# Six chained attention blocks on one core: the 128-row matmuls and transposes become pairs of 64-row ones, and all eight PSUM banks form one ring

## What is computed

```python
qp = (q @ Wq.T + bq).reshape(-1, H, seq, HD)       # kp, vp from the context
scores = jnp.einsum('bhqd,bhkd->bhqk', qp, kp)     # masks set scores to -inf
attn = jax.nn.softmax(scores / sqrt(HD), axis=-1)
out = jnp.einsum('bhqk,bhkd->bhqd', attn, vp).reshape(-1, seq, D)
y = x + out @ Wo.T + bo                            # then a layer norm
...
h = act(x @ w1.T + b1); y = x + h @ w2.T + b2      # 256 -> 1024 -> 256 in blocks 1 and 5
```

## Time and profile before

| | |
|---|---|
| median of 3 runs | 2486.88 us (2486.25 to 2492.78) |
| the profiled execution | 2489.72 us, of which the span from first to last instruction 2487.9 us |
| PE busy | 2393.9 us, 24352 matmuls |
| DVE busy | 1926.6 us |
| ACT busy | 1454.0 us |
| POOL busy | 1104.9 us |
| mean granted TensorE clock | 0.991 of full speed |

### The profile page before, as it was taken

The page is one execution under the profiler, slowest core; times in us unless marked ns, Lnnn a source line. Parts: engine busy times, 40 slices in busy tenths (PEclk is TensorE's granted clock), DMA queues, the critical chain, the costliest instruction groups (busy, mean ns, idle before and its releaser), DMA issues.

```text
span 2487.9 us, 63230 instructions
## 1 busy us (share of the span) xinstructions
PE 2393.9 (96%) x24352; PEld 1855.5 (75%) x24352; DVE 1926.6 (77%) x4308; ACT 1454.0 (58%) x2321; POOL 1104.9 (44%) x1606
## 2 busy tenths in 40 slices
PE   5999999999999989999999999999999999999997
PEld 4766767688888868878776666667777778888886
DVE  6888988877778877777788888878789876666662
ACT  1444444565555544455556677677677777666664
POOL 1333434444444433455445677786445443222220
PEclk8999999999999999999999999999999999999998
DMA  5453343222111111232222322222422221111120
GB/s 168 107 157 89 98 102 81 94 75 67 63 63 63 63 43 48 76 106 87 89 92 94 98 92 83 72 82 91 136 93 99 99 76 63 63 63 63 59 84 13
DMA packets 138379, 208.55 MB, mean 84 GB/s; under 512 B 43857, under 2 KB 52321, under 8 KB 138082
## 3 DMA queue, kind: packets, MB, share of 16 engines
q1 hardware_dynamic: 113506, 201.03, 24.7%
q0 software_dynamic: 24576, 3.49, 1.1%
HBM read 40.70 MB, written 4.19 MB: 18 GB/s over the span
## 4 chain that ended last, share of the span: by engine, by line
PE 68%; DVE 9%; issue 2%; ACT 1%; POOL 1%; DMA 0%; DVEq 0%; ACTq 0%
PE ps_pv L854 9%; PE ps_st L677 8%; PE ps_nat L659 7%; PE ps_misc L770 5%; PE ps_misc L886 3%; DVE mx L1307 3%; PE ps_misc L809 3%; PE ps_misc L919 3%; PE ps_misc L954 2%; PE ps_misc L903 2%; PE ps_misc L865 2%; PE ps_misc L955 2%; PE ps_misc L956 2%; PE ps_misc L921 2%; PE ps_misc L920 2%
## 5 line engine op out<-in xcount | busy, mean ns | idle before, releaser
L1037 ACT ACTIVATE pt<-ps_st 128x1024 f32<-128x1024 f32 (+1 forms) x768 | 760.3, 990 | 656.2 <-PE ps_st L677 367.4
L1428 POOL DMA_DIRECT2D q_st<-shifts_t x768 | 456.4, 599 | 1062.7 <-DVE shifts_t L1319 1062.2
L1307 DVE TENSOR_REDUCE mx<-ps_nat 128x4 f32<-128x1024 f32 x560 | 679.8, 1214 | 185.0 <-PE ps_nat L659 166.6
L659 PE MATMUL ps_nat<-k_st,q_st 64*128 64x256 f32 (+1 forms) x3072 | 353.8, 308 | 36.2 <-DVE mx L1307 20.1
L677 PE MATMUL ps_st<-q_st,k_st 64*128 64x256 f32 (+1 forms) x3072 | 366.5, 317 | 10.0 <-ACT pt L1037 6.2
L854 PE MATMUL ps_pv<-pt,vaug 128*32 128x256 f32 (+1 forms) x6144 | 374.5, 376 | 0.0
L677 PEld LDWEIGHTS ps_st<-q_st,k_st 64*128 64x128 f32 x3072 | 231.5, 185 | 145.2 <-issue 106.3
L659 PEld LDWEIGHTS ps_nat<-k_st,q_st 64*128 64x128 f32 x3072 | 233.4, 186 | 111.3 <-issue 63.9
L854 PEld LDWEIGHTS ps_pv<-pt,vaug 128*32 128x32 f32 x6144 | 171.8, 110 | 124.2 <-ACT pt L1037 7.1
L1086 ACT ACTIVATE hT<-ps_misc,cols 128x256 f32<-128x256 f32 x288 | 121.3, 477 | 130.3 <-PE ps_misc L921 72.4
L919 PE MATMUL ps_misc<-xF_hi,up_hi 128*128 128x256 f32 x512 | 158.1, 309 | 14.1 <-DVE qk L1185 10.9
(11 more groups left out here) (159 smaller groups left out, 5061.5 us busy)
## 6 DMA issues: line engine op xcount, KB each, us to landing
q_st<-qk SPq DMA_DIRECT2D x576, 128.0 KB
k_st<-qk SPq DMA_DIRECT2D x576, 128.0 KB, 2.1
q_st<-shifts_t POOLq DMA_DIRECT2D x768, 4.0 KB, 1.8
weights<-in_weights SPq DMA_DIRECT2D x19, 512.0 KB, 4.0
cT<-in_ctx_t SPq DMA_DIRECT2D x32, 256.0 KB, 2.8
cn<-in_ctx SPq DMA_DIRECT2D x32, 256.0 KB, 2.7
xT<-in_x_t SPq DMA_DIRECT2D x16, 256.0 KB, 3.2
xn<-in_x SPq DMA_DIRECT2D x16, 256.0 KB, 3.0
```

What stands on the lines that cost most here:

```text
L659: return nc.tensor.matmul(ps_nat[:, j, hf, 0:keys], lhs, rhs, start=hf == 0, stop=last)
L1037: nc.scalar.activation(pt[:, g % PT_SLOTS, :, 0:used], ps_st[:].rearrange("p j a b -> p j (a b)")[:, :, 0:used], ACT.Exp, scale=SCALE).the ...
L1307: last = nc.vector.reduce_max(out, ps_nat[:], AX)
L1428: nc.gpsimd.dma_start(rows[:, b], shifts_t[32 * b:32 * b + 32, i, :]).then_inc(split_in[rot][i], 16)
```

## The change

Every step named in `WIDE` now takes two neighbouring banks, and its matmuls are 64-row ones.

- `both_rows` replaces a 128-row matmul into one half of the output by two 64-row matmuls, on rows 0 to 63 and on rows 64 to 127. They write to different banks, so in part 0 rows 0 to 63 add into half 0 and rows 64 to 127 into half 1. In part 1 the two are swapped. Part 1 first waits (`rows_done`) until the last matmul of part 0 is done.
- `both_turns` replaces a transpose of 128x128 by two of 64 rows each, with 64 columns moved in place of 128.
- `ff2a` and `ff2` do the same over four parts, with a `rows_done` wait ahead of the second and the fourth.
- `otr` stays 128\*128 in blocks 2 and 3; `pvg` and `e0` stay 128\*32.
- The four PSUM tensors become one, `ps`, of eight banks. `Order` hands out banks, or pairs of neighbouring banks, oldest first, to all steps alike. `nat`, `st` and `pvg` are among them. PE waits for whatever step held the banks last.
- Readers take both banks with one access (two runs of 256, or blocks of 64). For `otr` of blocks 0, 1, 4 and 5 DVE now needs two reciprocals of 8 elements for one of 16, and four multiplications of 64 elements for one of 256 (blocks 1, 4, 5) or two of 128 (block 0).
- `STEPS` has new numbers throughout.

```diff
-MISC = 3
+BANKS = 8
+WIDE = {"nat": range(NA), "st": range(NA), "pq": (0, 1, 2, 3, 4, 5), "pk": (0, 1, 2, 3, 4, 5), "pvv": (0, 1, 2, 3, 4, 5), "opr": (0, 1, 4, 5),
+        "ff1": (1, 3, 5), "ff2": (1, 3, 5), "ff2a": (1, 5),
+        "xtr": (1, 2, 3, 4, 5), "xff": (1, 3, 5), "ctr": (3, 5), "otr": (0, 1, 4, 5), "ott": (1, 4, 5), "pvt": (0,)}
...
-    0: [("ldt", 0, -23.0722), ("pq", 0, -10.5145, {"a": -11.9187}), ("pql", 0, -10.1072), ("pk", 0, -8.6981, {"a":
+    0: [("ldt", 0, -15.0949), ("pq", 0, -11.609, {"q": -10.7939, "a": -10.4052}), ("pql", 0, -9.8317), ("pk", 0, -10.5429,
...
-                bank = next(b for b in turn if b not in held.values())
-                turn.remove(bank)
-                turn.append(bank)
+                taken = {b for banks in held.values() for b in banks}
+                age = {b: k for k, b in enumerate(turn) if b not in taken}
+                if wide(e):
+                    first = min((b for b in age if b + 1 in age), key=lambda b: (max(age[b], age[b + 1]), b))
+                    banks = [first, first + 1]
+                else:
+                    banks = [min(age, key=age.get)]
...
                 def open_bank(e, part=None):
-                    bank, count = win.bank[e]
-                    if count > 1 and part != 1:
-                        pe.wait_ge(misc_out[bank], count - 1)
-                    return ps_misc[:, bank, :]
+                    if part == 1 and wide(e):
+                        pe.wait_ge(rows_done, phases[e])
+                    if part != 1:
+                        for old in win.before[e]:
+                            if old[0] == "nat":
+                                pe.wait_ge(max_done, nth(old))
+                            elif old[0] == "st":
+                                pe.wait_ge(exp_done, nth(old))
+                            else:
+                                wait_out(pe, old)
+                    return ps[:, win.bank[e][0], :]
+
+                def both_turns(e, c, src):
+                    if not wide(e):
+                        return nc.tensor.transpose(ps[:, win.banks[e][0], P * c:P * c + P], src, ident[:])
+                    for g in range(2):
+                        rows = slice(GROUP * g, GROUP * g + GROUP)
+                        last = nc.tensor.transpose(ps[:, win.banks[e][g], GROUP * c:GROUP * c + GROUP], src[rows], ident[rows, rows])
+                    return last
+
+                def both_rows(e, swap, lhs, rhs, start, stop):
+                    out = halves_of(e)
+                    if not wide(e):
+                        return nc.tensor.matmul(out[:, swap, :], lhs[swap], rhs[swap], start=start, stop=stop)
+                    for g in range(2):
+                        half, rows = g ^ swap, slice(GROUP * g, GROUP * g + GROUP)
+                        last = nc.tensor.matmul(out[:, half, :], lhs[half][rows], rhs[half][rows], start=start and not swap,
+                                                stop=stop and bool(swap))
+                    return last
+
+                def half_done(e, last):
+                    phases[e] = len(phases) + 1
+                    last.then_inc(rows_done, 1)
...
-            for c in halves:
-                out, cut = bank[:, c * S:(c + 1) * S], slice((2 * i + c) * P, (2 * i + c + 1) * P)
-                for dk in range(2):
-                    nc.tensor.matmul(out, up_hi[dk][:, cut], xF_hi[:, dk, :], start=dk == 0, stop=False)
...
+            for dk in range(2):
+                w_hi, w_lo = [up_hi[dk][:, cut] for cut in cuts], [lo[:, dk, cut] for cut in cuts]
+                both_rows(e, part, w_hi, [xF_hi[:, dk, :]] * 2, dk == 0, False)
...
-                        link(nc.vector.reciprocal(rec[:, i], bank[:, :, :, HD]))
+                            for hf in range(2):
+                                last = nc.vector.reciprocal(own[:, hf], bank[:, hf, :, :, :, HD])
+                            link(last)
...
+                                for g in range(2):
+                                    src, by = bank[:, hf, :, g, :, 0:HD], own[:, hf, :, g].unsqueeze(3).to_broadcast([P, 2, 2, HD])
...
+                                    last = nc.vector.tensor_tensor(dst, src, by, ALU.mult)
```

More of the change, by code:

```diff
@@ L212, in plan @@
     return out
-MISC_KINDS = ("pq", "pk", "pvv", "pvt", "ctr", "e0", "otr", "ott", "opr", "xtr", "xff", "ff1", "ff2a", "ff2")
-RELEASE = {"len": "e0", "pql": "pq", "pkl": "pk", "xtl": "xtr", "xfl": "xff"}
+IN_BANKS = ("nat", "st", "pvg", "pq", "pk", "pvv", "pvt", "ctr", "e0", "otr", "ott", "opr", "xtr", "xff", "ff1", "ff2a", "ff2")
+RELEASE = {"pvout": "pvg", "len": "e0", "pql": "pq", "pkl": "pk", "xtl": "xtr", "xfl": "xff"}
 class Order:
@@ L230, in __init__ @@
         halved = {e for e, *_ in self.by["q"]}
-        self.kinds, self.bank = {}, {}
+        self.kinds, self.bank, self.banks, self.before, self.ready = {}, {}, {}, {}, {}
         for e in self.order:
             self.kinds.setdefault(e[0], []).append(e)
-        uses, held = [0] * MISC, {}
-        turn = list(range(MISC))
-        freeing = [s for s in self.by["d"] if s[0][0] in RELEASE and not (s[0][0] == "xfl" and attention(s[0][1]) == 5)]
+        uses, fills, held, last = [0] * BANKS, [0] * BANKS, {}, [None] * BANKS
+        turn = list(range(BANKS))
+        freeing = [s for s in self.by["a"] + self.by["d"]
+                   if s[0][0] in RELEASE and not (s[0][0] == "xfl" and attention(s[0][1]) == 5)]
         for e, part, *_ in sorted(self.by["p"] + self.by["q"] + freeing, key=lambda s: s[2:]):
@@ L806, in _ @@
                         wv = w("v" + str(a), D)
-                        for hf in halves:
-                            for dk in range(2):
-                                last = nc.tensor.matmul(bank[:, hf * D:(hf + 1) * D], src[:, dk, hf * P:(hf + 1) * P],
-                                                        wv[:, dk, :], start=dk == 0, stop=dk == 1)
+                        for dk in range(2):
+                            last = both_rows(e, part, [src[:, dk, hf * P:(hf + 1) * P] for hf in range(2)], [wv[:, dk, :]] * 2,
+                                             dk == 0, dk == 1)
                         filled(e, last, part)
@@ L841, in _ @@
                                 wait_out(pe, ("pvv", n, 0))
-                        if part != 1 and (count := nth(("pvout", n, i)) - 1):
-                            pe.wait_ge(ote_ready, count)
+                        bank = open_bank(e, part)
                         for c in halves:
@@ L882, in _ @@
                         wo = w("o" + str(a), D)
[L883 to L886 removed]
+                        for c in range(2):
+                            lhs = [(ot0 if a == 0 else ot)[:, c, th * P:(th + 1) * P] for th in range(2)]
+                            last = both_rows(e, part, lhs, [wo[:, c, :]] * 2, c == 0, c == 1)
                         filled(e, last, part)
@@ L940, in _ @@
                                 pe.wait_ge(d3_made, 1)
-                            for th in halves:
-                                out = bank[:, th * D:(th + 1) * D]
-                                nc.tensor.matmul(out, ones_b[:], d3_b[:], start=True, stop=False)
-                                for ch in range(2):
-                                    last = nc.tensor.matmul(out, hT[:, ch, th * P:(th + 1) * P], wd[:, ch, :], start=False, stop=ch == 1)
+                            both_rows(e, part, [ones_b[:]] * 2, [d3_b[:]] * 2, True, False)
@@ L957, in _ @@
-                            if kind == "ff2a" and i == 1:
+                                ch = 4 * quarter + c
+                                for at, down in ((4, down_hi), (4, lo), (0, down_hi)):
+                                    for g in range(2):
+                                        th, rows = g ^ swap, slice(GROUP * g, GROUP * g + GROUP)
+                                        last = nc.tensor.matmul(out[:, th, :], hT_r[rows, c + at, th * P:(th + 1) * P], down[rows, ch, :],
+                                                                start=step == 0 and c == 0 and at == 4 and down is down_hi,
+                                                                stop=step == 3 and c == 3 and at == 0)
```

333 lines of the change are left out of this document (178 added, 155 removed), and 114 rows, old and new, of the table STEPS.

## The result

| | before | after |
|---|---|---|
| median | 2486.57 us (2485.33 to 2492.78, 4 runs) | 2469.92 us (2468.02 to 2472.36, 4 runs) |
| ratio | | 0.9927, 95% interval 0.9912 to 0.9942 |
| the profiled execution | 2489.72 us | 2469.95 us, span 2468.1 |

The change makes the kernel 17 us faster. The forecast was 71 us, its time 2416 us; the range, 2335 to 2490, holds the result.

A forecast was written before the change was run, and what follows sets the result against it. The prediction took PE's issuing to bound the kernel, with DVE second. Its terms, -189 - 72 + 101 + 54 + 35, gave -71 us and a forecast of 2416 us, range 2335 to 2490.

The forecast's parts named there:

- What bounds the kernel: Whole kernel before: PE's order is priced at 2338 of 2488 us of span; DVE is second, at 84 to 88%.
- 1. Mode switches, -189: On PE, mode switches fall from 1647 to 658, saving 189 us.
- 2. Matmuls as pairs, 0: On PE, 64-row pairs cost as much as the 128-row matmuls, rounded or float32: 0 us.
- The fourth rival: On PE, float32 passes in series make each of 576 float32 parts 0.215 us later: +124, 2540 us; chance 0.14.
- 3. Transposes, -72: On PE, 1472 transposes become pairs at 0.060 us, from 0.109 us each, saving 72 us.
- the first rival: On PE, transposes gain nothing because the load of 128 columns sets the pace: about 2456 us; chance 0.20.
- 4. `rows_done`, +101: On PE, the new wait between parts costs 0.31 us at 297 adjoining parts, 93 us, plus 8 us at others.
- 5. The ring, +54: In PSUM's eight banks, four places for all steps make bank waits cost 54 us more; ends 0 and +90.
- The third rival: Readers eat the gain: ring binds DVE, ACT and PE, terms 5 and 6 at their ends and beyond: 2481; chance 0.06.
- 6. DVE, +35: In blocks 0 and 4, DVE's longer division makes it the bound, costing 35 us; ends 10 and 50.
- a sign of this term: For DVE's term: task periods near 24.7 in block 0 and 17.5 in block 4, DVE over 93% busy.
- The last sign named: In block 5, with the least to do for the readers, PE idle over 10% would show the forecast wrong.

## Why the prediction was wrong, step by step

**What bounds the kernel: right.** Taking the 120 us of `rows_done` off PE gave 113 us of time. DVE is second, and in block 0 as busy as PE.

**1. Mode switches, -189: right.** 321 became 131. (By the trace 1176 visits enter with full weights before, not 1159; that is 2 us.)

**2. Matmuls as pairs, 0: right.** Rounded pairs come 0.12 apart, and eight float32 passes take 4 x 0.216. The fourth rival, passes in series, is out: the two adjoining float32 parts above are 1.19 us apart, which is 0.86 and the pause.

**3. Transposes, -72: right.** A pair takes 0.06 us (1500.45 to 1500.79). The load still takes nearly what it took in the earlier trace rows, with 128 columns:

```profile
L678 PEld LDWEIGHTS ps<-ident,ote 64*128 64x128 f32 x1024 | 47.5, 138 | 11.4 <-issue 10.4 <-ACT ote L1119 0.5
```

So the 138 ns of a load don't set the pace of such pairs, and the first rival is out. The rule of the Trainium skill that I weighed there ("TensorE: Matmul & The Clock Gate", section "LDWEIGHTS (loading the stationary operand)"; an estimate of 107 ns a pair) doesn't agree with this trace. The rows of before couldn't decide it, as the forecast has it: transposes 0.109 us apart fit that rule as well. What the forecast left out is their price in banks, up to 69 us.

**4. `rows_done`, +101: right in kind, 19 short.** 158 rounded adjoining parts cost 58 us, 0.37 each, and 135 float32 ones 57, 0.42 each (four more wait for another engine too); I took 0.31 for both. The pause is 0.31 to 0.33 as worked out. What I missed is the start after it: the first pair of a part takes 0.20 and not 0.12 to the next. The parts further away cost 4 us in the account and 15 when laid beside the run without the wait; I had 8.

**5. The ring, +54: the step that failed.** The other waits rose by 125, or 115 by the second reading. DVE's extra work is 8 to 13 of that (next point), so the banks cost some 100 to 117, about twice my value and beyond my upper end of 90. I laid each bank wait against the priced distance from the filling step, with a reader that is always on time. The forecast says itself that "a reader that is itself late isn't in this sum", and its upper end, 36 us above, was too little for what the sum leaves out. What the runs show in its place is the second bank: with the transposes back in one bank each, up to 69 us of these waits go; with all but the scores in one bank, the other waits are 55 us, fewer than before.

Why the sum was too low for the pairs isn't shown. Late readers are the obvious reading. I looked for them first at ACT, which reads the results of `ff1`. Its idle time before them, in the last column, is

```profile
L1162 ACT ACTIVATE hT<-ps,cols 128x256 f32<-128x256 f32 x288 | 120.8, 471 | 163.6 <-PE ps L688 163.5
```

where the same group had 130.3 us before, also behind PE. ACT stands there until the second part of `ff1` is in, and any `st` behind it on ACT's list keeps its banks for as long. Block 1, which has this wait in every task, had 49 us of other waits in place of 13. But the runs speak against it as the main cause. The same row without the swap, with the feed-forward steps in 128 rows, and with the transposes in 128 rows:

```profile
L1157 ACT ACTIVATE hT<-ps,cols 128x256 f32<-128x256 f32 x288 | 121.5, 476 | 124.0 <-PE ps L686 122.6
...
L1160 ACT ACTIVATE hT<-ps,cols 128x256 f32<-128x256 f32 x288 | 121.1, 472 | 146.1 <-PE ps L683 120.6
...
L1160 ACT ACTIVATE hT<-ps,cols 128x256 f32<-128x256 f32 x288 | 120.9, 471 | 177.7 <-PE ps L686 177.7
```

In the first, ACT stands there for less than in the kernel before, and the other waits are 201 us, not fewer. In the second it stands for 18 us less, and they fall by 10. In the third it stands for 14 us more, and they fall by 69. So this idle time and PE's waits for banks don't go together, and which readers are late, and by how much, stays open. The third rival, readers eat it, was nearest in its time (2481) and right about the ring; its other half, DVE's term at its upper end, didn't come. It had 0.06.

**6. DVE, +35: right in place, too large.** I added 0.59 us an `otr` from the durations of single instructions. Successive multiplications overlap, though: busy time over count is 59.4/384 = 0.155 us, where the mean of one is 0.217. These rows answer to the earlier trace rows:

```profile
L1421 DVE TENSOR_TENSOR on<-ps,rec 128x64 f32<-128x64 f32 x384 | 59.4, 217 | 3.3
L1404 DVE RECIPROCAL rec<-ps 128x8 f32<-128x8 f32 x256 | 34.6, 177 | 31.6 <-PE ps L678 30.3
```

DVE's busy time grew by 19 us in place of the 71 that I had added up. At the 0.4 to 0.65 us of time for a us of DVE that the runs show, that is 8 to 13 us. The task periods, 24.43 and 17.39, came out near the 24.7 and 17.5 that I had named as a sign of this term; the sign was a poor one, since other waits filled them to the same length: without `rows_done` they are 23.96 and 16.93. The warning of the Trainium skill ("TensorEngine Tiling (Array Packing)", section "PSUM Bottleneck") fits the whole result better than my use of it for DVE alone. PE's busy time fell by 86 us, DVE's and ACT's rose by 19 each, and PE's waits other than `rows_done` grew by 125.

**The sum.** By the account term 4 is 19 us over its forecast, the banks some 59 over and DVE 23 under. That makes 55, the distance between 71 and 17 within the rounding. The last sign named, PE idle for over 10% in block 5, didn't come: it is busy for 95% of 2200 to 2400 us (190.08 of 200).

## What to carry to other kernels

Price the buffers that a faster form takes for longer, not only what it issues. Here twice the banks for a step returned about 40% of 262 us, and an order that avoided one wait ran into the other. A sum of fill times and read times gave only half of what the shared ring cost, so take such a sum as a lower end.

A wait of PE for its own last matmul cost a pause of 0.31 to 0.33 us here, 0.37 to 0.42 with the slow start after it. That is about as much as a change of mode there and back (0.39). Moving work between to cover it pays only if the buffers can be spared.

The busy time that more, smaller instructions add is busy time over count, from a row where they follow each other, and not the mean duration of one. For DVE's multiplications here that was 0.155 us where the mean is 0.217.

## What the hardware showed that I had not expected

- Pairs of 64-row transposes, each with a load of 128 columns, start 0.06 us apart, less than half of the 138 ns that one load takes.
- The two row halves often start 0.03 us apart rather than together (945.09 and 945.13 for one pair of `ff1`), at the same rate of a pair in 0.12 us:

```profile
945.09 0.36 PE L688 MATMUL ps<-xF_hi,up_hi 64*128 64x256 f32 x1
...
945.13 0.36 PE L688 MATMUL ps<-xF_hi,up_hi 64*128 64x256 f32 x1
945.29 0.32 PE L688 MATMUL ps<-xF_hi,weights_lo 64*128 64x256 f32 x2
```

- DVE's multiplications of 64 elements, 217 ns each, follow each other in 155.
